# First head's turned tiles through two banks, all but one read by ScalarE; low halves of weights and of values behind its keys and queries

## What is computed

```python
# x: (2, 1024, 128), 16 heads of 64
q = (x @ w_q).reshape(b, s, h, -1).transpose(0, 2, 1, 3)
kv = x @ w_kv
k, v = jnp.split(kv, 2, axis=-1)
q = _l2norm(q) * jnp.exp(scale)
k = _l2norm(k)
sim = jnp.einsum('bhid,bhjd->bhij', q, k)
attn = jax.nn.softmax(sim, axis=-1)
out = jnp.einsum('bhij,bhjd->bhid', attn, v)
```

## Time and profile before

| | us |
|---|---|
| median of 3 runs | 1032.54 |
| lowest and highest | 1030.79, 1032.74 |
| the profiled execution | 1036.26 |
| its span, first to last instruction | 1034.5 |
| TensorE busy in the span | 911.2 |
| VectorE, ScalarE, GpSimd busy | 732.8, 769.0, 512.2 |

### The profile page before, as it was taken

The page is one execution under the profiler, slowest core; times in us unless marked ns, Lnnn a source line. Parts: engine busy times, 40 slices in busy tenths (PEclk is TensorE's granted clock), DMA queues, the critical chain, the costliest instruction groups (busy, mean ns, idle before and its releaser), DMA issues. The chain is left out here.

```text
span 1034.5 us, 34747 instructions
## 1 busy us (share of the span) xinstructions
PE 911.2 (88%) x13676; PEld 857.5 (83%) x13676; DVE 732.8 (71%) x1427; ACT 769.0 (74%) x1281; POOL 512.2 (50%) x384
## 2 busy tenths in 40 slices
PE   3789999999999999999999997998989697899940
PEld 2678998998998999888989996997979587899840
DVE  6599989888988988988998993433469877410113
ACT  5689998998998988988989974444565375587840
POOL 5465655655655564654678821322418372053433
PEclk8799999999999999999999997998999798899985
DMA  8400000000000000000001020533201002023221
GB/s 258 131 3 3 23 3 22 3 3 22 3 3 23 3 2 23 2 3 23 8 10 37 14 63 1 180 99 88 57 27 32 11 32 69 14 66 99 65 58 45
DMA packets 43563, 42.13 MB, mean 41 GB/s; under 512 B 5648, under 2 KB 37392, under 8 KB 43408
## 3 DMA queue, kind: packets, MB, share of 16 engines
q1 hardware_dynamic: 39312, 31.51, 10.2%
q0 software_dynamic: 4096, 8.40, 2.8%
HBM read 25.60 MB, written 14.29 MB: 39 GB/s over the span
## 5 line engine op out<-in xcount | busy, mean ns | idle before, releaser
L699 ACT ACTIVATE Pr<-SC,nesc,esc 128x1024 f32<-128x1024 f32 x256 | 310.2, 1212 | 32.9 <-PE SC L511 22.9
L815 DVE TENSOR_TENSOR Pl<-Pr 128x1024 f16<-128x1024 f32 x224 | 293.2, 1326 | 39.7 <-ACT Pr L699 38.1
L510 PE MATMUL SC<-QK 128*128 128x256 f16 x1024 | 238.8, 274 | 1.0 <-ACT QK L681 1.0
L511 PE MATMUL SC<-QK 128*128 128x256 f16 x1024 | 238.9, 274 | 0.0
L536 PE MATMUL OP<-V,Pr 128*128 128x65 f16 x2048 | 214.4, 192 | 6.1 <-DVE Ob L838 5.9
L538 PE MATMUL OP<-V,Pr 128*128 128x64 f16 x2048 | 215.3, 195 | 0.0
L540 PE MATMUL OP<-V,Pl 128*128 128x65 f16 x2048 | 214.1, 191 | 0.0
L536 PEld LDWEIGHTS OP<-V,Pr 128*128 128x128 bf16 x2048 | 191.0, 97 | 12.8 <-issue 8.7
L538 PEld LDWEIGHTS OP<-V,Pr 128*128 128x128 bf16 x2048 | 190.0, 97 | 2.6
L540 PEld LDWEIGHTS OP<-V,Pl 128*128 128x128 f16 x2048 | 190.7, 99 | 0.0
L1066 POOL TENSOR_TENSOR stk<-nrm,stk 128x512 f16<-128x512 f32 x64 | 75.2, 1176 | 139.8 <-DVE stk L797 139.8
(11 more groups left out here) (234 smaller groups left out, 2175.0 us busy)
## 6 DMA issues: line engine op xcount, KB each, us to landing
ys<-yb SPq DMA_DIRECT2D x92, 64.0 KB
w_or_rows<-xs SPq DMA_DIRECT2D x12, 384.0 KB, 4.2
wst<-in_up SPq DMA_DIRECT2D x8, 512.0 KB
xs<-zero SPq DMA_DIRECT2D x2, 1472.0 KB, 13.1
scratch<-in_up SPq DMA_DIRECT2D x4, 576.0 KB
wd<-in_wd SPq DMA_DIRECT2D x4, 576.0 KB
wd<-in_wd SPq DMA_DIRECT2D x4, 512.0 KB
QK<-in_wqkv SPq DMA_DIRECT2D x4, 384.0 KB, 7.4
```

The lines of the kernel that those rows point to most:

```text
L510: eng.matmul(out, QK[:, b, 1, key:key + P], rhs, start=True, stop=False)
L511: mm = eng.matmul(out, QK[:, b, 2, key:key + P], rhs, start=False, stop=True)
L699: eng.activation(Pr[:, n % PB, :, :], SC[s % 2][:, :, :], ACT.Exp, bias=nesc[:, hd:hd + 1], scale=esc[:, hd:hd + 1]).then_inc(s_exps, 1)
L815: eng.tensor_tensor(Pl[:, n % PB, :, :].rearrange("p a b -> p (a b)"), pr, high(pr)[:, 1::2], ALU.subtract).then_inc(s_low_probs, 1)
```

## The change

Four edits, all in step 0 (h = 0) and its surroundings:

1. A new function `turn_bank(h, j)`: in step 0 odd pairs are turned into `SC[1]`, the bank of the second score buffer, even ones into `M1`.
2. In step 0 ScalarE reads pairs 0, 1, 2, 3, 4, 5 and 7, VectorE only pair 6. `m1_free` now asks in step 0 for `j - 1` reads by ScalarE, so for the pair before the last. The counts of the later steps are moved to fit.
3. VectorE makes the low halves of weight chunks 1 to 3 after its read of pair 6, just ahead of `heads`.
4. GpSimd makes the four low halves of values after the four low parts of queries and keys.

```diff
+        def turn_bank(h, j):
+
+            if h == 0 and j % 2:
+                return SC[1][:, 0:2, :].rearrange("p a b -> p (a b)")
+            return M1[:, :]
+
...
             def m1_free(h, j, i, s, here=0):
 
-                wait(eng, s_turned_read_vector, 4 if h else (j + 1) // 2)
-                wait(eng, s_turned_read_scalar, 8 * h - 4 + j if h else j // 2)
+                if h == 0:
+                    wait(eng, s_turned_read_scalar, j - 1)
+                else:
+                    wait(eng, s_turned_read_vector, 1)
+                    wait(eng, s_turned_read_scalar, 8 * h - 1 + j)
                 wait(eng, s_out_turned_read, 8 * i + out_before(s + here, turn_slot))
...
-                m1 = M1[:, :].bitcast(F16)
+                m1 = turn_bank(h, j).bitcast(F16)
...
-                    wait(eng, s_turned_read_vector, 4)
-                    wait(eng, s_turned_read_scalar, 8 * h + 4)
+                    wait(eng, s_turned_read_vector, 1)
+                    wait(eng, s_turned_read_scalar, 8 * h + 7)
...
-                               M1[:, :].bitcast(F16)[:, 0:6 * P].rearrange("p (k c) -> p k c", k=3),
+                               turn_bank(h, j).bitcast(F16)[:, 0:6 * P].rearrange("p (k c) -> p k c", k=3),
...
-            for j in range(1, PJ, 2):
+            for j in (0, 1, 2, 3, 4, 5, 7):
                 read_transposes(0, 0, j)
...
                 copy_keys(0, 0, g)
-                if g:
-                    low_weights(g)
-                    read_transposes(0, 0, 2 * (g - 1))
             read_transposes(0, 0, 6)
+            for c in range(1, WCH):
+                low_weights(c)
             heads(eng, slot)
...
                     inverse_norms(0, 0, g + 1)
+                low_parts(0, 0, g)
+            for g in range(4):
                 low_values(0, 0, g)
-                low_parts(0, 0, g)
             heads(eng, slot)
```

## The result

The changed kernel took **1025.49 us** (median of 5 runs, 1023.78 to 1026.90) against 1030.79 us for the kernel before (5 runs, 1030.21 to 1032.74). The ratio is 0.9945, with a 95% interval of 0.9932 to 0.9958: 4.3 to 7.0 us less. The profiled execution took 1024.61 us, its span is 1022.9 us.

What follows compares the result with a forecast made beforehand. Ahead of the first score, GpSimd's chain and VectorE's queued single-bank reads were taken as the bound. First score 34.64 to 28.2 gives -6.4 us, low weights cost 0: 1032.54 - 6.4 = 1026.1 us, range 1023.5 to 1029.0.

Steps and rivals of the forecast that it cites:

- my own signs: Checks named beforehand, among them head 0's last low part done at 25 to 26 and first score at 27.5 to 29.
- GpSimd's chain: Inverse norms and low parts before the first score: without the values between, last low part ends at 25.6 instead of 28.26.
- collisions that I had put on the clamps: VectorE's clamp for group 2 collides with low parts 0, ending about 17.45; group 3's follows low parts 1 at 20.45.
- The lock rule: VectorE and GpSimd share ports under an exclusive lock per instruction; forecast accepted it for low parts, not for inverse norms.
- longer collisions: Rival, chance 0.07: VectorE also held up under inverse norms before the first score; score at 29.3, gain 5.3, about 1027.4 us.
- Two banks, read by ScalarE: Turning head 0's tiles: turn overlaps the previous read, ScalarE's reads don't queue; first score at 28.2 instead of 34.64.
- Low weights: VectorE's three low weights behind the read of tile 6 end at 31.4, hidden with nothing left over; cost 0.
- Carrying on: After the first score: the 6.4 us gain shifts the whole pipeline if no fixed date catches it.
- starving rival: Chance 0.05: TensorE's instruction fetch queues behind the zero fill until about 34.6; nothing gained, 1032 us.
- clock rival: Chance 0.13: TensorE's clock holds or returns earlier around the last turns and first scores; gain 8.5, 1024.0 us.
- full case of that rival: First two slots of scores escape half clock, worth about 1.6 us on ScalarE's path.
- slower rival: Chance 0.03: the stretch from 600 to 1034 us loses clock, 0.87 instead of 0.90; 12 us more, leaving 1038.

Runs made afterwards that it cites:

- norms ahead: The changed kernel with each GpSimd inverse norm issued one place earlier in its list; 1029.35 us, ratio 0.9931 to the kernel before.
- one bank: The changed kernel with all turned pairs of step 0 through M1 again, readers as in the change; 1029.29 us, ratio 0.9968 to the kernel before.
- second profile of the change: The changed kernel, nothing altered, measured again on another occasion; 1030.31 us against 1035.51 for the kernel before, ratio 0.9944.
- high parts on ScalarE: The changed kernel with the high-part casts of groups 2 and 3 made by ScalarE instead of VectorE; 1024.68 us, ratio 0.9939 to the kernel before.
- values between: The changed kernel with GpSimd's low values back between the low parts; 1027.55 us, ratio 0.9951 to the kernel before.
- values last only: The kernel before with only GpSimd's low values moved behind the low parts; 1029.30 us, ratio 0.9972 to the kernel before.

## Why the prediction was right

**The size.** Forecast -6.4 us, 1026.1; measured -5.3, 1025.49, with the kernel before at 1030.79 instead of the 1032.54 that I had subtracted from. That the absolute number came so close is partly luck: the median of the kernel before came down by 1.75 us with two more runs, and against that the gain itself was 1.1 us too large in the forecast, 1.0 us of it in the start. Two of my own signs were missed by a little: the last low part (25 to 26 said, 26.63 measured) and the first score (27.5 to 29 said, 29.20 measured).

**GpSimd's chain.** Predicted end 25.6, measured 26.63. The term that was wrong is the inverse norm: I took 1.64 for each in its new place, and of the three behind the first, the second ended 0.67 us later (16.95 instead of 16.28: it began 0.15 us later, behind a clamp that came 0.16 us later than in the profile before, and took 2.19 instead of 1.66), and the others took 2.09 and 2.08: 1.56 us too much in all. Against it, the collisions that I had put on the clamps didn't come, so low parts 2 started 1.09 us late (23.24 instead of 22.15). From there the chain took what I had said, 3.39 us for 3.45, but not as I had said: low parts 2 took 1.15 instead of 1.59, because with the values gone GpSimd gets ahead, and low parts 3 then waited 1.09 us for VectorE, whose normalization took 1.63 instead of 0.69. I had the rows for both outcomes in hand (0.69 and 0.43 under an inverse norm that had begun) and the earlier trace rows even had an inverse norm of 2.01, which I used only as an upper end. What I read from them, that the two don't disturb each other, was true only of the order in which those had started.

**The lock rule.** I set the rule of the Trainium skill (SBUF — State Buffer, "SBUF: two separate sides") against the row at 14.69 and went by the row. Both turn out half right. An inverse norm that has begun doesn't hold VectorE up for its length: with norms ahead, a normalization began at 20.30, 0.17 us into an inverse norm, and took 0.69 us. So the loss of about 0.5 us per cast that I had worked out from the rule didn't happen. But a normalization that has begun holds up the inverse norm, by 0.4 to 0.5 us each time, and low parts and normalizations do block each other nearly whole, as the rule says: 1.63 = 0.69 + 0.94 of low part. The rival "longer collisions" (first score at 29.3, gain 5.3) had the right number, 29.20, and the wrong mechanism.

**Two banks, read by ScalarE.** From the last low part to the first score 2.6 predicted, 2.57 measured. Right in each step, and the experiment with one bank shows that the second bank is needed for the gain of GpSimd's order to arrive: edit 4 alone gave 1.22 us, edits 1 to 3 alone 3.01 (21.64 - 18.63), all four 5.49.

**Low weights.** Predicted to end at 31.4, ended at 31.46, by luck: they began 1.0 us later than predicted (28.08 instead of 27.1) and took 3.38 us instead of 4.3. I had written that nothing was left over; since the first score came 1 us later too, VectorE had 0.95 us left, and twice the work cost nothing, thanks to the cover that I had named behind it.

**Carrying on.** Right: no fixed date caught the gain. The instruction fetch that had fallen between 33 and 34 us fell between 31 and 32 us now, inside the zero fill, and TensorE had no wait for it. The starving rival is out. The clock rival was partly true: the first two turns ran at full clock (0.49 and 0.50 us instead of 0.76 and 0.82), the later ones didn't, and the clock came back at 33 us, 3.8 us behind the first score instead of 4.5. That is of the size of the 0.4 us by which the end of attention moved more than its start. In the second profile of the change the clock came back only 5.1 us behind the first score, and the end of attention lies 0.4 us further behind the first score (584.0 instead of 583.6). The full case of that rival, the first scores at full clock, appeared in the kernel with norms ahead and was worth 1.3 to 1.7 us there; I had put it at 1.6.

**The slower rival.** The granted clock from 600 us on was 0.90 again. What does vary is the length of that stretch, 408 to 416 us between profiles, a spread larger than this change; only medians over several runs show the change.

## What to carry to other kernels

When a pipeline can't start before a preparation is complete, cut all chains of the preparation at once: here GpSimd's order alone gave 1.2 us of the start and the other edits alone (banks, reader, low weights) 3.0, together 5.5. Before a duration is taken over to a new order, look at what ran beside it and which of the two had started first; between VectorE and GpSimd both directions have their own price. And work that nobody waits for belongs behind the chain of the engine that is the bound: the values on GpSimd were worth 2.5 us, the later weights on VectorE, which wasn't the bound any more, 0.2. Check the new place too: twice the weights' length there cost nothing.

## What the runs showed of the hardware

- An inverse norm (GpSimd, power, 128x8) took 1.63 to 1.67 us when no two-input operation or cast of VectorE was running at its start, and 2.01 to 2.12 us when such a two-input operation (a normalization, or VectorE's own low part) was already running; 1.81 to 1.82 when it was a cast. In all of them the excess over 1.66 us was some 0.16 us less than what VectorE's operation still had to go: 0.15 for 0.32, 0.37 for 0.53, 0.43 for 0.59, 0.46 for 0.62.
- With starts within a tenth of a microsecond it was either: 1.66 and 1.64 us (the kernel before at 14.61, high parts on ScalarE at 14.64), or 2.19 us (the change at 14.76, norms ahead at 16.87). VectorE's normalization took 0.69 to 0.73 us inside an inverse norm that had begun.
- A GpSimd low part (128x512) of 1.15 us made a normalization that came within 0.1 us behind it take 1.62 to 1.63 us instead of 0.69. Where low values (0.65 us) had begun 0.07 us ahead of the normalization (the kernel with values between), it took 1.13 us. In both cases the normalization ended 0.55 us behind the GpSimd operation. A low part that began with 0.58 us of the normalization still to go took 1.60 us.
- VectorE's copy from PSUM (L806, 0.55 us) took 0.54 to 0.56 us in every profile, beside GpSimd's low values too, and a low part that began 0.02 us behind it (23.61, values last only) took its 1.15 us.
- TensorE's granted clock at the first score was 0.50 in every profile but that with norms ahead, where it was 1.00 from 28.90 us on.
